# An early tile table in two parts, a choice behind two query quarters, and low weights made in other steps

## What is computed

```
h = conv8x8(norm([x, four shifted copies of x]) * gamma + beta) + b      # 64 images x 169 tokens x 128
n = layernorm(h); q, k, v = n @ Wqkv                                      # 8 heads of 64
q', k' = exp(q*scale @ proj), exp(k @ proj)
h = h + (q' @ (k'^T v)) / (q' @ sum(k') + 1e-6) @ Wout + bout             # per image and head
n = layernorm(h); gate = n @ Wg; each token keeps its top 2 of 8 experts, softmax over the two
h = h + sum over the two of  w_e * ((silu(n @ W[e]) * (n @ V[e])) @ W2[e])
```

## Time and profile before

| | before |
|---|---|
| median of 3 runs | 1143.21 us (1141.93 to 1144.71) |
| the profiled execution | 1143.8 us, its span in the profile 1142.0 us |
| TensorE matmuls busy | 1089.6 us, 95% of the span |
| VectorE, GpSimd, ScalarE busy | 77%, 54%, 49% |
| steps, then tiles | steps to about 675 us, tiles from there |

### The profile page before, as it was taken

One profiled execution on the slowest core, in us unless ns is written; L12 is line 12 of the kernel. 1 busy time (PEld: TensorE's weight loads), 2 busy tenths in 40 slices (PEclk: granted clock), 3 DMA queues, 4 the chain that ended last, 5 costly groups with the idle time before them and its releaser, 6 DMA issues.

```text
span 1142.0 us, 30063 instructions
## 1 busy us (share of the span) xinstructions
PE 1089.6 (95%) x8628; PEld 924.8 (81%) x8629; DVE 882.1 (77%) x3333; ACT 561.5 (49%) x1307; POOL 614.4 (54%) x656
## 2 busy tenths in 40 slices
PE   3999999999999999999999979999999999999996
PEld 3677777777777777777776669999999999999996
DVE  5568887887888878878868677777777777777774
ACT  3545535536345354363333425555555555555552
POOL 0103545445445444454444466676767676677675
PEclk9999999999999999999999999999999999999998
DMA  8270131311301213011110424343443443444443
GB/s 166 51 203 22 38 74 32 80 30 33 81 31 35 77 30 82 27 36 30 33 30 31 114 72 75 47 58 53 55 51 53 55 56 53 53 53 54 54 56 31
DMA packets 76012, 65.53 MB, mean 57 GB/s; under 512 B 12338, under 2 KB 66802, under 8 KB 75926
## 3 DMA queue, kind: packets, MB, share of 16 engines
q0 software_dynamic: 32704, 24.99, 15.7%
q1 hardware_dynamic: 43078, 39.16, 13.9%
q10 hardware_dynamic: 144, 0.32, 0.1%
HBM read 32.72 MB, written 31.71 MB: 56 GB/s over the span
## 4 chain that ended last, share of the span: by engine, by line
PE 79%; DVE 11%; issue 3%; DMA 3%; ACT 1%; SPq 1%; POOL 1%; DVEq 0%; POOLq 0%; another core or an unknown queue 0%; ACTq 0%
PE bank L1472 20%; PE bank L1495 13%; PE bank L690 7%; PE bank L739 5%; PE bank L752 5%; PE bank L620 4%; PE bank L726 4%; PE bank L728 3%; PE bank L727 3%; PE bank L745 3%; PE bank L477 2%; PE bank L708 2%; DVE rparts L930 2%; PE bank L613 2%; DMA out_rows<-yo,dest 2%
## 5 line engine op out<-in xcount | busy, mean ns | idle before, releaser
L1666 POOL DMA_INDIRECT out_rows<-yo,dest x184 | 312.5, 1699 | 138.0 <-issue 103.7
L1472 PE MATMUL bank<-xT_e,wv 128*128 128x256 f32 x2208 | 288.5, 286 | 2.4 <-DVE xT_e L1583 2.2
L1472 PEld LDWEIGHTS bank<-xT_e,wv 128*128 128x128 f32 x2208 | 270.8, 189 | 2.9 <-DVE xT_e L1583 2.4
L1349 POOL DMA_INDIRECT sorted_rows<-xrow_all,sloti x192 | 192.0, 1000 | 77.5 <-issue 58.0
L1553 ACT ACTIVATE sil<-bank 128x256 f32<-128x256 f32 x368 | 141.0, 385 | 168.3 <-PE bank L1472 149.5
L1495 PE MATMUL bank<-w,hid 128*128 x1472 | 181.4, 277 | 4.4 <-DVE hid L1590 4.0
L1495 PEld LDWEIGHTS bank<-w,hid 128*128 128x128 f32 x1472 | 173.0, 193 | 5.8 <-issue 5.7
L1572 DVE TENSOR_TENSOR wv<-wv_all,wv 128x1024 fp32r<-128x1024 f32 x92 | 113.3, 1232 | 65.4 <-PE bank L1472 51.2
L1590 DVE TENSOR_TENSOR hid<-sil,bank 128x256 f32<-128x256 f32 x368 | 143.8, 417 | 25.2 <-ACT sil L1553 21.3
L1256 ACT ACTIVATE attn<-bank 128x256 f32<-128x256 f32 x128 | 49.5, 387 | 161.5 <-issue 123.4
L1534 ACT CAST wv<-wv_all 128x1024 fp32r x92 | 96.2, 1046 | 30.7 <-issue 28.2
(11 more groups left out here) (216 smaller groups left out, 1816.0 us busy)
## 6 DMA issues: line engine op xcount, KB each, us to landing
xr<-sorted_rows SPq DMA_DIRECT2D x92, 130.0 KB
raw<-in_x SPq DMA_DIRECT2D x64, 84.5 KB
raw<-in_x SPq DMA_DIRECT2D x60, 78.0 KB
out_rows<-attn SPq DMA_DIRECT2D x64, 58.5 KB
sorted_rows<-xrow_all,sloti POOLq DMA_INDIRECT x192
out_rows<-yo,dest POOLq DMA_INDIRECT x184
wv_all<-in_L_ffn_W SPq DMA_DIRECT2D x8, 256.0 KB, 5.1
wv_all<-in_L_ffn_V SPq DMA_DIRECT2D x8, 256.0 KB, 5.3
```

The source lines that it names most:

```text
L1349: po.indirect_dma_start(sorted_rows, bass.IndirectOffsetOnAxis(sloti[:, p, j, ch:ch + 1], 0), xrow[:, p, j, ch], None).then_inc(s(f"scatte ...
L1472: q = pe.matmul(bank[fc][:, TT * m:TT * m + TT], wv[:, w, w_, m, cols], xT[:, p, x_], start=(w_ + x_ == 0), stop=(w_ == 1))
L1666: po.indirect_dma_start(out, bass.IndirectOffsetOnAxis(dest[:, p, a:a + 1], 0), yo[:, p, a], None, compute_op=ALU.add).then_inc(s(f"added{ ...
```

## The change

Three things are moved on VectorE; no arithmetic is added or removed.

- `early_table` becomes `early_counts` (the nine instructions on the counts, L1044 to L1054) and `early_table` (the eleven behind them). The first stands in step 30 and the second in step 31, both ahead of the statistics of the step, where before all 20 stood at the end of step 30.
- In step 32 the choice of pair 29 stands behind the first two query quarters instead of ahead of them.
- `low_w` of tile 1 is made in step 32 instead of 33, and that of tile 2 in step 33 instead of the step of tile 1.

```diff
-                if n == NPAIR:
-                    choose(md)
...
                 if c:
                     normalise(1)
+                if n == NPAIR:
+                    choose(md)
                 front(0)
...
+                if n == NPAIR:
+                    expert_vector(ve, "weights", range(1, 2))
                 if n == NPAIR + 1:
-                    expert_vector(ve, "weights", range(1, 2))
+                    expert_vector(ve, "weights", range(2, 3))
...
                 if d and a:
                     normal_rows()
+                if n == NEARLY_PAIRS + 2:
+                    early_counts()
+                if n == NEARLY_PAIRS + 3:
+                    early_table()
...
-                if n == NEARLY_PAIRS + 2:
-                    early_table()
...
         def step(t, h, p, w, more, prev, more2):
-            if more and not (isinstance(t, int) and t < 1):
+            if more and not (isinstance(t, int) and t < 2):
                 low_w(t + 1, (w + 1) % 4)
```

More of the change, by code:

```diff
@@ L1030, in best, with early_chain, early_counts @@
                 ve.wait_ge(s("gap_whole"), m + 1)
-            def early_table():
+            early_link = [0]
+            def early_chain(q):
+                early_link[0] += 1
+                q.then_inc(s("early_step"), 1)
+                ve.wait_ge(s("early_step"), early_link[0])
+            def early_counts():
+                chain = early_chain
                 ve.wait_ge(s("colsum_ready"), 4 * NG)
                 ve.wait_ge(s("counts_ready"), NEARLY_PAIRS)
[L1036 to L1043, removed]
+                n_ = slice(0, R1)
                 chain(ve.tensor_tensor(early_has, counts[n_].unsqueeze(2).to_broadcast([R1, E, FIRST_TILES]),
@@ L1054, in early_table @@
                 chain(ve.tensor_tensor(early_more, early_of[:, 1:E + 1], early_of[:, 0:E], ALU.subtract))
+            def early_table():
+                chain = early_chain
                 chain(ve.tensor_tensor(early_past, K("tile")[0:1].unsqueeze(2).to_broadcast([1, FIRST_TILES, E]),
```

## The result

The changed kernel takes 1135.13 us (median of 6 runs, 1133.98 to 1135.84), the kernel before beside it 1141.95 (6 runs): the ratio is 0.9934, 95% interval 0.9921 to 0.9947, a gain of 6.8 us. The prediction said 6.4 us off and 1137.4 us, range 1135.3 to 1140.6.

What follows compares the result with a forecast made beforehand. TensorE bounds the expert tiles, so gains lie in its waits ahead of them. 2.54 (table) + 1.4 (choice) + 2.5 (low weights and clock, held by SyncE) = 6.4 us off 1143.8 gives 1137.4 us, range 1135.3 to 1140.6.

Steps and rivals of the forecast that it cites:

- the base: Starting time of the sum: the profiled execution's own 1143.8 us, taken as 0.6 above the median of 1143.21.
- the choice: Step 32: pair 29's choice behind two query quarters lets the rank product start earlier; 1.4 us, bounds 1.0 to 1.5.
- the third part: Moved low weights of tiles 1 and 2 with the clock gain: 2.65 us together, taken as 2.5, bounds 0.8 to 2.65.
- The early table: Steps 30 and 31: splitting the table removes TensorE's wait for the inverse sums; 2.54 us, at least 2.2.
- Low weights: Tile 1's step loses one VectorE product and its register read, 1.9 us; the product fits a gap in step 32.
- The clock: Tile 1's step: with less TensorE idling no fall to half rate, saving VectorE's wait before L1596; 0.75 us.
- SyncE: Tile 4's rows can move 0.8 us, tile 5's rows go at 692.5 at best; holds the gain to about 2.5.
- The clock falls elsewhere: Shifted waits cause one more unhidden half-rate stretch on TensorE, +1.7 us, 1139.1 us; chance 0.15.
- The adds swallow the third part: SyncE or GpSimd's adds absorb the gain; if tile 5's rows move only 0.8 us, 1139.1 us; chance 0.10.
- A shared port: Step 32: tile 1's VectorE product holds GpSimd by 0.8 us on the path of the roots, 1138.2 us; chance 0.05.
- no change: GpSimd's chain of adds is anchored elsewhere, so all 6.4 us come back, about 1143.5; 0.07 together with a shortfall case.
- slower: TensorE's clock stays low over steps 33 and 34, adding 10.8 us, 1148.2 us; chance 0.03.

Runs made afterwards that it cites:

- s_after1: The changed kernel with no edit, a third execution for its stages; a single run, 1133.29 us.
- e_table: The kernel before with only the early tiles' table split over steps 30 and 31; 1138.59 us, ratio 0.9967.
- e_after: The changed kernel with no edit, measured a second time; 1136.64 us (8 runs), ratio 0.9945 to the kernel before.
- e_low: The kernel before with only the low weights of tiles 1 and 2 moved; 1139.35 us, ratio 0.9975.
- e_same: The kernel before with no edit, repeated; 1140.82 us against 1142.0, ratio 0.999.
- s_before1: The kernel before with no edit, once more for its stages; a single run, 1139.81 us.

## Why the prediction was right in its gain and wrong in its time

**The step that failed is the base**, "6.4 us off the profiled execution's own 1143.8 us". That execution was taken as 0.6 above what is typical, by the median of three, and the sum started from it. It stands 1.85 above the median of six, 1141.95: the three runs at hand had by chance a high median. All later runs of this kernel agree with the six (medians 1142.0, 1142.38 and 1142.6, one run of 1141.19). Step 30 started at 595.34, where the median of the seventeen profiles is 593.72 (1.6 more), and from step 31 on it took 153.26 against 152.7 (0.55 more, by the unlaid wait of 0.75 us). That is 2.2, somewhat more than the 1.85 to be explained, and both are outside the change. The sum of 6.4 on 1141.95 gives 1135.55, 0.4 from what was measured. That 0.4 is the second part of the miss: two of the sum's terms came out too small, and the measured values lie above the upper bounds that the prediction gave (the choice 1.58 against 1.5, the third part 2.8 against 2.65). Either error alone would have left the time inside the range.

The start goes with the loads of the first 30 us. The first 30 and 60 us of the slow start of before and of the quickest of the changed kernel, s_after1:

```profile
0.00:30.00 30.00, 11.69 (x66) 10.45 (x68) 17.50 (x45) 10.89 (x16) 2.79 (x9) 1.00 0.86 164
0.00:60.00 60.00, 39.02 (x212) 30.47 (x215) 32.69 (x100) 28.07 (x52) 6.92 (x16) 1.00 0.55 108
```

```profile
0.00:30.00 30.00, 15.01 (x76) 13.32 (x78) 19.91 (x52) 10.78 (x16) 3.89 (x10) 1.00 0.79 193
0.00:60.00 60.00, 42.35 (x260) 32.89 (x262) 33.05 (x102) 29.74 (x58) 6.90 (x16) 1.00 0.47 114
```

In 30 us the queues moved 164 GB/s in the one and 193 in the other, and by then TensorE had worked 11.69 and 15.01 us: the 3.2 us between the two starts of step 30 (595.34, 592.16). Over all seventeen, the seven that started past 595 moved 163 to 166 GB/s in their first 30 us, and the three ahead of 592.3 moved 183 to 193. That they go together was read, not tried. It is not all of it: in two of the seven late ones, e_table and e_after, the granted clock also fell for 3.4 us at 57.7 and 58.2 us.

**The early table, 2.54**: 2.54, wherever the clock stayed up in step 31. The cover of 1.1 us is there (L916 waits 1.08). Left out was what the wait puts at risk: two executions lost 1.3 and 1.5 more behind it, which the split takes away too.

**The choice, 1.4**: 1.58. The rank product stands at 637.88, right behind the choice, as said; the quarter and the choice overlapped a little more than my 0.51 and 1.88 (quarters 0.83 for two, 635.16 to 635.99, the choice 1.83).

**Low weights, 1.9 of work**: 2.2. The 0.32 and 0.35 of the stages on both sides make the third part 2.8, but they are not theirs alone: e_table has the first without moving any low weights, and e_low lost 0.16 in the second. In step 32 the product fitted with 0.32 us to spare, of 0.25 to 0.60 said.

**The clock, 0.75**: some 0.3, between nothing and 0.6. Its price in the sum was the 0.75 us before L1596, and that wait is not the clock's: e_same and s_before1 have the same stretch at half rate and no such wait.

**SyncE, which was to hold the third part to 2.5**: it didn't. Ahead of tile 4's rows it no longer waits (1.37 us in e_same), so there it does bind, and these rows moved 1.7 us. But ahead of tile 5's rows it still waits for the table, the last row here:

```profile
SPq L116 <- DVE meta_ L1587: 15.8, 5, 4.7
...
SPq L447 <- DVE table L1612: 3.3, 1, 3.3
```

Tile 5's rows went out 0.96 us behind the table, as before, 2.7 us nearer to step 33's start than in e_same. That is three times the 0.3 us that the prediction gave the registers there. Of the sum's three terms one was right and two were too small, by 0.2 and 0.3: 6.4 stands against 6.9. That the third came so near is partly luck, since a clock term that was too large stood against work that was sized too small.

**The rivals.** "The clock falls elsewhere" happened in place: in two of four executions of the changed kernel, at 0.2 to 0.3 us and not 1.7, since TensorE waits for VectorE there in any case (L585). "The adds swallow the third part" happened in part: GpSimd is full from 681.19 us on and VectorE waits 1.78 us, but TensorE stands only 0.63 us for it. "A shared port" happened in small: in step 32 VectorE's product took 1.38 us beside GpSimd's copy and 1.23 elsewhere, and the copy 1.30 in place of 0.52 in the step behind:

```profile
644.58 1.30 POOL L1378 COPY xrow_all<-xrow_all 128x384 f32<-128x384 f32 x1
```

GpSimd's scatters show it more sharply. In the seventeen traces 40 of them begin while VectorE makes such a product (1.23 us), and 37 of these end 0.83 to 0.87 us behind the product's end, wherever in it they began, and so take up to 2.0 us in place of 0.96. The Trainium skill's page "SBUF — State Buffer", section "SBUF: two separate sides", has the rule, and these scatters agree with it: the one that comes second waits for the other's end. The 0.15 us by which the product of step 32 grew, though it began 0.44 us before the copy, is not explained by that rule. The copy's delay of 0.8 us fell on GpSimd, which then waited 0.6 us for the statistics all the same. Nothing of the cases "no change" and "slower" was seen.

## What to carry to other kernels

A prediction of a fraction of a per cent stands on its base as much as on its terms: read the untouched part ahead of the change as well, and set the time of the profiled execution against the median of more runs than three before you subtract from it (three gave 1143.21 here, six 1141.95). Price a stretch at half rate by what the next wait leaves of it; slow products that run into another engine's wait cost only the rest. And lay a wait to a cause only where the trace names one: "remote" beside something slow is not evidence. Compare the numbers of records of two traces before you compare their stages.

## What the runs showed of the hardware

Step 30, with the same work ahead of it in all seventeen executions, started between 591.65 and 596.83 us, and its start went with the rate of the first loads, 163 to 193 GB/s over 30 us. Behind the same wait of 2.2 us in step 31 TensorE's granted clock fell to 0.50, 1.2 GHz, in two of eight executions, and stayed at 1.00, 2.4 GHz, in six; each stretch lasted 3.4 us. In the changed kernel it fell in two of four executions behind three waits of 0.48, 0.80 and 0.60 us, and stayed up behind the same three in the other two. A VectorE product of two SBUF inputs and a GpSimd copy at the same time took 0.15 and 0.78 us longer than alone, and a GpSimd scatter that began beside such a product ended 0.83 to 0.87 us behind it in 37 of 40 cases.
